# Moving the normalisation of the local softmax from VectorE to ScalarE in a two-branch transformer kernel

## What is computed

```
def local_attention(q, k, v):
    ...
    sim = jnp.einsum('bhwid,bhwjd->bhwij', bq, bk)
    ...
    sim = jnp.where(mask, -jnp.finfo(sim.dtype).max, sim)
    attn = jax.nn.softmax(sim, axis=-1)
    out = jnp.einsum('bhwij,bhwjd->bhwid', attn, bv)
```

## Time and profile before

| What | us |
|---|---|
| median of 3 runs | 2380.59 |
| lowest and highest of them | 2374.51 and 2381.43 |
| the profiled execution | 2383.1 |
| its span, first to last instruction | 2381.2 |
| PE busy | 2168.9 (91%) |
| DVE busy | 1827.8 (77%) |
| ACT busy | 1148.8 (48%) |
| POOL busy | 934.9 (39%) |

### The profile page before, as it was taken

One profiled execution on the slowest core, in us unless ns is written; L12 is line 12 of the kernel. 1 busy time (PEld: TensorE's weight loads), 2 busy tenths in 40 slices (PEclk: granted clock), 3 DMA queues, 4 the chain that ended last, 5 costly groups with the idle time before them and its releaser, 6 DMA issues.

```text
span 2381.2 us, 48786 instructions
## 1 busy us (share of the span) xinstructions
PE 2168.9 (91%) x15282; PEld 1867.6 (78%) x15282; DVE 1827.8 (77%) x5354; ACT 1148.8 (48%) x2734; POOL 934.9 (39%) x941
## 2 busy tenths in 40 slices
PE   4889989999899989999899989989999999999997
PEld 3778877877787877877787877878888888888786
DVE  5667887778767787688767887777888888888885
ACT  2234443344334443344333443346677676776764
POOL 3334453345434453345433453343333333333331
PEclk8778998889978898899888998889999999999999
DMA  4000000000000000000000000012111111111110
GB/s 162 11 13 17 20 18 14 15 19 18 14 13 19 15 18 14 13 21 18 14 13 15 19 18 14 14 51 69 33 36 33 33 37 32 36 33 33 37 33 25
DMA packets 71792, 64.37 MB, mean 27 GB/s; under 512 B 12444, under 2 KB 64984, under 8 KB 71608
## 3 DMA queue, kind: packets, MB, share of 16 engines
q1 hardware_dynamic: 71736, 63.65, 8.9%
HBM read 38.45 MB, written 12.58 MB: 21 GB/s over the span
## 4 chain that ended last, share of the span: by engine, by line
PE 50%; DVE 30%; issue 13%; DMA 3%; ACT 1%; DVEq 1%; SPq 1%; POOL 1%; POOLq 0%; ACTq 0%
PE bank L1327 38%; PE bank L1332 7%; PE bank L1339 5%; DVE prob L940 4%; DVE prob L926 4%; DMA x_shift<-x 2%; DVE rot L1250 2%; DVE sq_sum L1196 2%; DVE qk_sum L1209 2%; DVE rot L1228 1%; DVE hid L1257 1%; DVE v_mix L1223 1%; DVE mix_work L982 1%; DVE h_n L1158 1%; DVE h_n L1156 1%
## 5 line engine op out<-in xcount | busy, mean ns | idle before, releaser
L1327 PE MATMUL bank<-hT_n,w_s 128*128 128x128 f32 x3072 | 389.6, 279 | 0.5 <-ACT hT_n L711 0.5
L1327 PEld LDWEIGHTS bank<-hT_n,w_s 128*128 128x128 f32 x3072 | 364.9, 193 | 15.2 <-issue 10.8
L1332 PE MATMUL bank<-wqkv_s,xT 128*128 128x512 f32 x1152 | 319.4, 413 | 24.0 <-DVE xT L1104 18.4
L741 ACT ACTIVATE prob<-prob,row_min 128x256 f32<-128x256 f32 x512 | 256.1, 503 | 63.8 <-DVE row_min L926 61.5
L1327 PE MATMUL bank<-w_s,hid 128*128 128x256 f32 x768 | 284.5, 489 | 0.2 <-DVE hid L1257 0.2
L1332 PEld LDWEIGHTS bank<-wqkv_s,xT 128*128 128x128 f32 x1152 | 207.8, 192 | 81.8 <-DVE xT L1104 27.1
L711 ACT ACTIVATE k_dec<-bank 128x512 f32<-128x512 f32 x32 | 19.1, 598 | 515.6 <-PE bank L1339 515.6
L940 DVE TENSOR_SCALAR prob<-prob,row_inv 128x256 f32<-128x256 f32 x512 | 224.3, 480 | 9.2 <-DVE row_inv L935 0.2
L926 DVE CUSTOM_DVE_ANT_0 prob<-bank,table,inv_norm 128x256 f32<-128x256 f32 x512 | 226.2, 478 | 2.7 <-issue 2.7
L633 POOL TENSOR_TENSOR rot_other<-raw,rot_t 128x256 f32<-128x256 f32 x256 | 186.5, 761 | 93.3 <-ACT raw L711 93.3
L596 POOL TENSOR_TENSOR inv_norm<-sq_clip,half_neg 128x16 f32<-128x16 f32 x64 | 188.7, 2948 | 63.6 <-DVE sq_clip L1199 63.6
(11 more groups left out here) (182 smaller groups left out, 4699.8 us busy)
## 6 DMA issues: line engine op xcount, KB each, us to landing
k_prev<-k_carry SPq DMA_DIRECT2D x32, 224.0 KB, 2.5
x_s<-in_L_attn_x SPq DMA_DIRECT2D x32, 128.0 KB, 2.1
rot_s<-in_rotary SPq DMA_DIRECT2D x64, 64.0 KB, 2.0
s_between_passes<-s_out SPq DMA_DIRECT2D x32, 128.0 KB, 1.7
x_between_layers<-x SPq DMA_DIRECT2D x32, 128.0 KB, 1.7
x_s<-x_between_layers SPq DMA_DIRECT2D x32, 128.0 KB, 2.0
xn<-x_between_layers SPq DMA_DIRECT2D x32, 128.0 KB, 2.1
s_out<-s_between_passes SPq DMA_DIRECT2D x32, 128.0 KB, 2.1
```

What stands on the lines that cost most here:

```text
L741: ins = act.activation(prob[:, h, :], prob[:, h, :], ACT.Exp, bias=row_min[:, c:c + 1], scale=-1.0, accum_out=row_sum[:, c:c + 1])
L1327: return pe.matmul(out, lhsT, rhs, start=first, stop=last)
L1332: ins = pe.matmul(out, halved(left[:, a]), halved(right[:, b]), start=first and n == 0, stop=last and n == 2)
```

## The change

ACT gets a function `weigh`, which multiplies `prob` by the reciprocal row sum with an ACTIVATE of the function Copy whose scale is the column `row_inv`, two per step of heads. DVE's `weigh` becomes `invert` and keeps only the reciprocals. PE's `att_turn` waits for ACT's event `n...` in place of DVE's. Nothing changes in the DMAs.

```diff
-        att_act = Steps(sem("att_act"), "ea0 ea1 eb0 ta0 ta1 eb1 pva tb0 tb1 pvb")
-        att_dve = Steps(sem("att_dve"), "sa0 sa1 sb0 ra0 na0 ra1 na1 rb0 nb0 sb1 "
-                        "rb1 nb1 la lb x1")
+        att_act = Steps(sem("att_act"), "ea0 ea1 eb0 na0 na1 nb0 ta0 ta1 eb1 nb1 pva tb0 tb1 pvb")
+        att_dve = Steps(sem("att_dve"), "sa0 sa1 sb0 ra0 ra1 rb0 sb1 "
+                        "rb1 la lb x1")
...
+            def weigh(step, a):
+
+                s = list(STEP_HEADS).index(step)
+                act.wait_ge(att_dve.sem, att_dve.at("r" + step, a))
+                for j, h in enumerate(STEP_HEADS[step]):
+                    c = 2 * s + j
+                    ins = act.activation(prob[:, h, :], prob[:, h, :], ACT.Copy, scale=row_inv[:, c:c + 1])
+                ins.then_inc(att_act.done("n" + step), 1)
...
                     exps("a1", a)
                     exps("b0", a)
+                    weigh("a0", a)
                 if proj is not None:
                     act.wait_ge(proj_pe.sem, proj_pe.at("k", proj))
...
                         .then_inc(mlp_act.done("ht"), 1)
+                if a is not None:
+                    weigh("a1", a)
                 if proj is not None:
                     act.wait_ge(proj_act.sem, proj_act.at("k", proj))
                     act.activation(rot[:, :], raw[:, :], ACT.Square).then_inc(proj_act.done("square"), 1)
                 if a is not None:
+                    weigh("b0", a)
                     for k in range(2):
                         turned(f"a{k}", k, a, att_bank[1 + k])
...
                     act.activation(p_tanh, p_lin, ACT.Tanh, scale=0.5).then_inc(mix_act.done("tanh"), 1)
+                if a is not None:
+                    weigh("b1", a)
...
-            def weigh(step, a):
+            def invert(step, a):
...
                    .then_inc(att_dve.done("r" + step), 1)
-                dve.wait_ge(att_dve.sem, att_dve.at("r" + step, a))
-                for j, h in enumerate(STEP_HEADS[step]):
-                    c = 2 * s + j
-                    ins = dve.tensor_scalar(prob[:, h, :], prob[:, h, :], row_inv[:, c:c + 1], None, ALU.mult)
-                ins.then_inc(att_dve.done("n" + step), 1)
...
-                pe.wait_ge(att_dve.sem, att_dve.at("n" + step, a))
+                pe.wait_ge(att_act.sem, att_act.at("n" + step, a))
```

More of the change, by code:

```diff
@@ L1161, in body @@
                     scores("b0", a, att_bank[2])
-                    weigh("a0", a)
+                    invert("a0", a)
                 if mix is not None:
@@ L1167, in body @@
                 if a is not None:
-                    weigh("a1", a)
-                    weigh("b0", a)
+                    invert("a1", a)
+                    invert("b0", a)
                 if a is not None and mix is None:
@@ L1219, in body @@
                 if a is not None:
-                    weigh("b1", a)
+                    invert("b1", a)
                 if mix is not None:
```

## The result

The changed kernel takes 2497.37 us in the median of 4 runs (2474.45 to 2502.88), the kernel before 2381.01. The ratio is 1.0474 with a 95% interval of 1.0404 to 1.0544: slower by 116 us (96 to 130 by the interval) where +60 was forecast. The profiled execution took 2502.88 us, its span is 2501.1.

What follows compares the result with a forecast made beforehand. In the second pass ACT's sequence without a pause was taken to bind, level with the chain through DVE and PE. Terms +74 (copies), +19 (clock) and -34 (first pass) gave +59 us; forecast 2441 us, range 2395 to 2500.

Steps and rivals of the forecast that it cites:

- the price of the second pass: Second pass: three pairs in ACT's sequence without a pause cost 2.3 us a unit, +74 us; clock drops add +19.
- 1.2 us in half the units for the clock: Second pass: PE's new pauses drop TensorE's clock in half the units, 16 * 1.2 = +19 us.
- the prediction's lower bound: Second pass: three pairs priced by the plain copy cost 1.7 us a unit, +54 us.
- b1 in the second pass: Second pass: b1's pair and the GELUs come 3.4 us later, covered by v projection, MLP matmuls and b1 transposes.
- the sign of the first pass: First pass: the output projection and the unit's rest come 1.15 us earlier, 30 units, -34 us.
- The mechanism of the first pass: First pass: DVE's rotation delays POOL's `gate`, freeing line 1244; line 1250 waits once; 1.15 us a unit won.
- b1's stall going through whole: Rival, first pass: DVE's late chain ends 2.3 us earlier in 31 units, -71; 2364 us in all; chance 0.08.
- The clock rival: Rival, second pass: the clock drops in every unit, +38 instead of +19; 2461 us in all; chance 0.13.

Runs made afterwards that it cites:

- e3: The changed kernel with ACT weighing in the second pass only and DVE multiplying in the first: 2472.59 us, ratio 1.0408 to the kernel before.
- e7: The changed kernel with only the b0 pair on ACT, in the second pass only: 2405.52 us, ratio 1.0101 to the kernel before.
- e4: The changed kernel with plain copies on ACT, without the scale column, so nothing is normalised: 2471.05 us, ratio 1.0396 to the kernel before.
- e6: The changed kernel with only the b1 pair on ACT, in the second pass only: 2431.79 us, ratio 1.0212 to the kernel before.
- e1: The changed kernel plus 24 one-column memsets on DVE in the setup, moving the loop's code back: 2438.18 us, ratio 1.0263 to the kernel before.
- f12: The kernel before without b1's multiplications in units 0 to 30, on no engine (two heads unnormalised): 2455.01 us, ratio 1.0325.
- e2: The kernel before plus 104 one-column memsets on DVE in the setup, nothing else: 2421.16 us, ratio 1.0200.
- f10: The changed kernel with only b1 on ACT, first pass, units 0 to 30, plus 6 memsets: 2330.28 us, ratio 0.9821 to the kernel before.

## Why the prediction was right, and where it was wrong

**Right: the price of the second pass.** Forecast were 2.3 us a unit for three pairs of 0.77, and 1.2 us in half the units for the clock. Measured: 25.17 - 22.89 = 2.28 for pairs of 0.80, and 26.43 - 25.17 = 1.26 in 18 of 29. The sum over 32 units is 98 us against 93. e3, with nothing else changed, confirms it (2473 measured, 2478 expected), e7 that a pair in that stretch passes most of its length on (0.71 of 0.80 us), e4 that it is the length which counts: plain copies cost 1.73 us a unit, and the prediction's lower bound had 1.7.

**Right by luck: b1 in the second pass.** I costed it at nothing, and named the v projection and the MLP matmuls as its cover. But alone it costs 1.68 us there (e6), so the cover seems to be the lateness of the other three pairs, which no run tests by itself. I had not asked where the reciprocal stands in DVE's list.

**Wrong: the sign of the first pass**, -34 us in the sum. The step that failed is not one of those listed but one that is missing: the change takes 24 instructions out of DVE's list ahead of the loop and 24 out of its body, and I took the loop to run as before. It came with 12 pauses of 2.8 to 3.0 us. Over the 27 units PE is idle for 28 us more than in e1 (124.7 against 96.7) and busy for 42 us more at a lower clock (1217.5 against 1175.5, granted 0.87 against 0.90). In the whole time that is 59 us by the medians, 50 against the runs beside each (e1). With this taken out the first pass wins (48.67 - 47.12) * 27 = 42 us, where the sum had 34. That 2497 still lies inside the range of 2395 to 2500 is luck: without the pauses e1 took 2438 us, and the rest is a term that I had not named. The Trainium skill's "Runtime: NRT & Kernel Launch", section "Instruction fetch mechanics", says that a taken branch whose target is no longer in the fetched window forces a fetch before the engine goes on. The pauses and the packets agree with it; which place of the code makes it happen no run here settles, beyond that 24 instructions switch it off and 104 switch it on.

**The mechanism of the first pass** was half right. A unit of the changed kernel shows DVE's and POOL's items as I had placed them:

```profile
1079.65 1.63 DVE L1238 TENSOR_TENSOR rot<-raw,rot_t 128x1024 f32<-128x1024 f32 x1
1082.85 0.42 DVE L1102 TENSOR_TENSOR oT<-bank,oT 128x256 fp32r<-128x256 f32 x1 [1.57 <-ACT oT L711]
...
1084.33 0.69 DVE L1254 TENSOR_TENSOR mix_work<-mix_work,k_prev 128x512 f32<-128x512 f32 x1
1085.09 1.75 DVE L1260 TENSOR_TENSOR rot<-rot,inv_norm 128x512 f32<-128x512 f32 x1
```

The sum of line 1244 that took 1.75 us takes 0.69 (it is line 1254 here), the one behind it still takes 1.75, and the rotation, now beside POOL's product, 1.63. But PE gives half of it back, here in its timeline, with waits for the late GELU (1.31 us) and for ACT's copy of v (0.46 us); the output projection no longer waits for DVE, as it did in rows 11:

```profile
1082.60 1.16 PE L1337 MATMUL bank<-hT_n,w_s 128*128 128x128 f32 x8 [1.31 <-ACT gel L839]
...
1087.23 0.65 PE L1349 MATMUL bank<-table,rot 128*128 128x128 f32 x4 [0.46 <-ACT v_loc L711]
...
1088.90 1.69 PE L1342 MATMUL bank<-wo_s,oT 128*128 128x256 f32 x12
```

So a unit wins 0.6 us at an equal clock, where I had 1.15. Over the 27 units of e1 PE is idle for 15 us less than in the kernel before (96.7 against 111.4), where the sum had 31. The other 27 of the 42 us come through the clock (busy 1175.5 against 1202.6), above all in the 8 units that miss the half clock. The sum had no such term, so that e1's 2438 us lies near the forecast 2441 is luck in this part.

**The rivals.** The one on the faster side, b1's stall going through whole, is refuted as a mechanism by f12: with b1's multiplications on no engine and no late GELU, PE is idle for 4.0 us a unit against 4.1, not 2.3 us less. The measured 2497 lies at the upper end of the range for a reason that no rival had. The clock rival came closest, with 0.62 of the units instead of all.

## What to carry to other kernels

An engine that is idle on average can have a stretch without a pause, and what is put into that stretch is paid whole: look for it in the timeline of each pass, and ask of each moved item what stands in front of the value it waits for on the other engine. A change in the number of instructions moves the code of every loop behind it; so compare the instruction packets of the two pages, and the time from a loop's branch to its first item, before any other cause is believed. Here that was worth 50 to 59 us, more than two of the three terms that were argued about. And a choice can be made per stage: the same edit costs 2.3 to 3.5 us a unit in one pass and wins 1.6 in the other. Where a clock falls in some units and not in others, sort the units by it before a gain or a loss is put down to work: the granted clock and PE's idle time tell the two apart.

## What the hardware showed that I had not expected

- A loop's back branch on DVE takes 0.28 us or 2.8 to 3.0 us, the long ones with 5 instruction packets of 8 KB each, by the place of the code alone (e1, e2).
- With the same matmuls a unit takes 42.7 us without half clock or 48.8 us with 13.7 us of it (f10). One moved pair changed which units have it, from all 27 to 19; which shift does that is open.
- Leaving out 2.3 us of DVE work a unit made the kernel 78 us slower: DVE and POOL hold each other up in another order, PE waits as long as before at other places, and the granted clock of the first pass falls from 0.88 to 0.82 (f12).
